# Four chained layers on one core: ScalarE evicts the first quarter of layer 0 ahead of rounding the shared gate weights, and VectorE rounds the shared up weights

## The reference

```
x = x + (x @ W_base.T + b_base + 2 * sum_e cond[b,e] * (x @ A_e.T) @ B_e.T)      # layer 0
x = x + x @ (sum_g cond[b,g] * weight_g * mask).T + bias                           # layer 1
x = x + sum over the top 2 experts e of cond[b]: w[b,e] * mlp_e(x)  + mlp_shared(x) # layer 2
x = x + (silu(x @ up_e.T + b) * (x @ gate_e.T + b)) @ down_e.T + b                 # layer 3, e = argmax cond[b]
mlp(x) = (gelu(x @ gate) * (x @ up)) @ down,   gate, up: 128x512, down: 512x128
```

## Time and profile before

| | |
|---|---|
| median of 3 runs | 85.93 us (85.29 to 86.2) |
| the profiled execution | 85.2 us, its span 83.9 us |
| PE busy in the span | 97% |
| DVE, ACT, POOL busy | 58%, 38%, 19% |
| granted TensorE clock | 1.000 of full speed in the whole span |

### The profile page before, as it was taken

How to read it: one execution, slowest core, us unless ns; L and a number is a source line. 1 busy time by engine, 2 the same in 40 slices (tenths; PEclk the granted TensorE clock), 3 DMA queues, 4 the chain that set the end, 5 groups by cost and what they waited for, 6 DMA issues and landing times.

```text
span 83.9 us, 1937 instructions
## 1 busy us (share of the span) xinstructions
PE 81.0 (97%) x620; PEld 77.0 (92%) x620; DVE 48.5 (58%) x115; ACT 31.5 (38%) x59; POOL 15.8 (19%) x20
## 2 busy tenths in 40 slices
PE   6999999999999999999999999999999999999990
PEld 6979988888889989999999999999999999999980
DVE  1489699754337996437438428446465564652271
ACT  6500996865558301122121221221302402316560
POOL 3020577589666600000000000000000000000000
DMA  1997000899990000985869899889899889805202
GB/s 21 334 392 279 2 0 0 240 413 390 420 388 35 0 0 15 308 272 182 314 220 323 238 324 331 277 264 309 268 368 336 311 308 311 331 19 120 99 0 66
DMA packets 5336, 18.51 MB, mean 221 GB/s; under 512 B 592, under 2 KB 1744, under 8 KB 5328
## 3 DMA queue, kind: packets, MB, share of 16 engines
q1 hardware_dynamic: 5040, 17.62, 61.1%
q10 hardware_dynamic: 288, 0.79, 2.4%
HBM read 17.88 MB, written 0.52 MB: 219 GB/s over the span
## 4 chain that ended last, share of the span: by engine, by line
PE 97%; DVE 0%; issue 0%; DVEq 0%
PE bank L690 34%; PE bank L700 17%; PE bank L713 9%; PE bank L727 5%; PE bank L662 4%; PE bank L654 4%; PE bank L670 4%; PE bank L586 3%; PE bank L592 3%; PE bank L622 2%; PE bank L677 2%; PE bank L678 2%; PE bank L680 2%; PE bank L610 2%; PE bank L601 2%; DVE out_sb L507 0%
## 5 line engine op out<-in xcount | busy, mean ns | idle before, releaser
L690 PE MATMUL bank<-x_t,pair_w 128*128 128x128 f32 (+1 forms) x256 | 31.0, 275 | 0.0
L690 PEld LDWEIGHTS bank<-x_t,pair_w 128*128 128x128 f32 x256 | 29.9, 192 | 0.1
L301 ACT ACTIVATE gelu<-bank 128x512 f32<-128x512 f32 x24 | 14.2, 598 | 31.6 <-PE bank L690 27.8
L478 DVE SCALAR_TENSOR_TENSOR hid<-gelu,wsel,bank 128x512 f32<-128x512 f32 x16 | 12.0, 748 | 18.5 <-PE bank L690 18.5
L700 PE MATMUL bank<-hid,pair_w 128*128 128x128 f32 x128 | 16.9, 275 | 0.0
L700 PEld LDWEIGHTS bank<-hid,pair_w 128*128 128x128 f32 x128 | 15.6, 192 | 0.1
L265 POOL TENSOR_TENSOR hid_l<-hid,hid_h 128x512 fp32r<-128x512 f32 x8 | 10.2, 1284 | 4.2 <-ACT hid_h L329 4.2
L476 DVE TENSOR_TENSOR hid<-gelu,bank 128x512 f32<-128x512 f32 x8 | 5.5, 688 | 6.1 <-ACT gelu L301 3.6
L713 PE MATMUL bank<-x_t,w 128*128 128x128 f32 x64 | 8.5, 276 | 0.0
L713 PEld LDWEIGHTS bank<-x_t,w 128*128 128x128 f32 x64 | 7.8, 192 | 0.0
L305 ACT ACTIVATE tanh<-half 128x256 f32<-128x256 f32 x6 | 2.5, 417 | 10.0 <-DVE half L514 10.0
(11 more groups left out here) (70 smaller groups left out, 76.4 us busy)
## 6 DMA issues: line engine op xcount, KB each, us to landing
pair_w<-in_skill SPq DMA_DIRECT2D x16, 768.0 KB, 5.5
w<-in_layer SPq DMA_DIRECT2D x8, 384.0 KB, 5.2
rest_sb<-in_rest SPq DMA_DIRECT2D x1, 661.0 KB, 3.9
x_t<-in_x SPq DMA_DIRECT2D x1, 512.0 KB, 5.4
shared_sb<-in_shared ACTq DMA_DIRECT2D x1, 512.0 KB, 5.2
out_x<-out_sb SPq DMA_DIRECT2D x8, 64.0 KB, 4.1
shared_sb<-in_shared ACTq DMA_DIRECT2D x1, 256.0 KB, 5.4
head_sb<-in_head SPq DMA_DIRECT2D x1, 164.0 KB, 2.3
```

What stands on the lines that cost most here:

```text
L301: act.activation(gelu[:, n, :], ps[:, :], ACT.Gelu_apprx_tanh).then_inc(gelu_ready, 1)
L478: dve.scalar_tensor_tensor(hid[:, n, :], gelu[:, n, :], wsel[:, bass.DynSlice(weight, 1)], u_ps[n][:, :], ALU.mult, ALU.mult).then_inc(hid ...
L690: mm = pe.matmul(ps[:, S * t:S * (t + 1)], pair_w[:, slot, n, 128 * t:128 * (t + 1)], x2_t[:, columns(b)], start=True, stop=True)
```

## The change

Three edits. On ACT, the eviction of quarter 0 stands before the rounding of the gate weights, which now stands between quarters 0 and 1; the rounding of the up weights leaves ACT. On DVE, a `tensor_copy` from `shared_sb` to `shared_h` does it, behind the last instruction of the routing and before the first `stream2`. The semaphore `sh_high`, which counted three roundings of one engine, becomes three semaphores, one for each block.

```diff
-        sh_high, sh_low = sem("sh_high"), sem("sh_low")
+        sh_high, sh_low = [sem(f"sh_high{n}") for n in range(3)], sem("sh_low")
...
-                    pool.wait_ge(sh_high, n + 1)
+                    pool.wait_ge(sh_high[n], 1)
...
-                    act.activation(shared_h[:, n, :], shared_sb[:, n, :], ACT.Copy).then_inc(sh_high, 1)
+                    act.activation(shared_h[:, n, :], shared_sb[:, n, :], ACT.Copy).then_inc(sh_high[n], 1)
...
+                act.wait_ge(rest_landed, 16)
+                stream1(0)
                 round_shared(0)
-                act.wait_ge(rest_landed, 16)
-                for n in range(4):
+                for n in range(1, 4):
                     stream1(n)
-                round_shared(1)
                 round_shared(2)
...
                 rank_second()
+                dve.wait_ge(gate_up_in, 16)
+                dve.tensor_copy(shared_h[:, 1, :], shared_sb[:, 1, :]).then_inc(sh_high[1], 1)
...
-                        pe.wait_ge(sh_high, m + 1)
+                        pe.wait_ge(sh_high[m], 1)
```

## The result

The changed kernel is **slower**: 86.44 us median of 22 runs (85.48 to 87.69), against 85.65 us of 22 runs of the kernel before (84.89 to 86.83). The ratio is **1.0098, 95% interval 1.0074 to 1.0123**, so about 0.8 us were lost, where 0.12 us were forecast as gained. A second measurement, 12 runs, gave 1.0072 (1.0025 to 1.0119).

The account below looks back on a forecast made before the run. PE, busy 97% of the span, was taken as the bound, so only holes could be closed: -0.14 us at the first seam, +0.02 at the next, 0 elsewhere, -0.12 us from the 85.93 median to 85.8 us; range 85.2 to 86.7.

Parts of the forecast that it names:

- the sum's last sentence: After the changed stretch all work is PE's own and shifts as a whole, so the -0.12 us reaches the end.
- The cast's price: Up rounding on DVE at one element per cycle, 0.69 us; lower bound 0.33 us at half streaming price.
- The first rival: The CAST on DVE waits behind POOL's first low part for the shared port: +0.7 us, about 86.6 us; chance 0.27.
- its dearer form: The CAST waits for POOL and still needs the full 0.53 us of streaming: +0.96 us.
- the rounding's end: ACT's gate rounding, put behind quarter 0's eviction, ends at 9.28, 0.12 us ahead of POOL's first low part; costs nothing.
- the first seam: Between layers 0 and 1 on PE, evicting quarter 0 first closes a hole: 0.14 us gained.
- the close fit of quarter 1: Quarter 1, ready at 9.65, is just in time for layer 1's fifth load at 9.77; a miss loses some hundredths.
- the zero for the semaphores: Three semaphores for one leave the waits and their places the same: no cost.
- The earlier up rounding: Up block ready at 10.18 instead of 10.97; POOL's second low part ends 0.36 us earlier, so PE's waiting load is freed.
- the third rival: Shared weights' DMA lands late in some runs, where the change saves more: up to 0.4 us, 85.5 us; chance 0.05.

Follow-up runs that it names:

- scalar_form: Changed kernel with VectorE's rounding of the up weights as a tensor_scalar (multiply by 1.0) instead of the cast: 86.44 us, ratio 1.0087.
- after_again: The changed kernel measured and traced again with no edit: 86.0 us, ratio 1.0072.
- pad_dve: Kernel before plus one 128x1 copy into a spare tile on VectorE, nothing else: 86.37 us, ratio 1.0071.
- dve_less: Changed kernel without one repeated wait (for base_ready) on VectorE, so its program there is as long as before: 85.89 us, ratio 1.0016.
- early_pad8: Changed kernel with the cast moved ahead of the routing's second half and eight more 128x1 copies on VectorE: 85.54 us, ratio 0.9974.
- cast_only: Kernel before with only the up rounding moved from ScalarE to VectorE (semaphore split), ScalarE still rounding the gate first: 86.58 us, ratio 1.0114.
- lost_less: cast_only without VectorE's repeated wait for base_ready, so its program there is as long as before: 86.08 us, ratio 1.0062.
- evict_only: Kernel before with only ScalarE's order changed, quarter 0 evicted ahead of the gate rounding; up rounding stays on ScalarE: 85.80 us, ratio 1.0008.
- split_only: Kernel before with only the semaphore sh_high split into three, no instruction moved: 85.60 us, ratio 1.0006.
- early_less: Changed kernel with the cast ahead of the routing's second half and without VectorE's repeated wait for base_ready: 85.54 us, ratio 1.0019.

## Why the prediction was wrong

**The step that failed is the sum's last sentence**: "All later work is PE's own, at full pace, and shifts as a whole." It is right for TensorE to within 0.1 us in most traces: from the expert matmuls to the last block its chain takes 54.84 to 54.96 us in fourteen of the sixteen, and 55.06 and 55.08 in scalar_form and after_again; why it is longer in these is open. It is wrong for the span, which ends with a store. I costed the added instruction by its time on VectorE and never by its place in the program. pad_dve shows that the mere instruction costs 0.6 us (1.0071), and dve_less that taking one away elsewhere brings the changed kernel back to 1.0016.

That the delay of the store is made by the code packet itself is read from the packets' records in all 16 traces, counted from the start of the last `out_sb`. In the seven with a last wait of 0.9 to 1.1 us, the packet starts at 1.47 us or later, or, in early_pad8, 0.85 us ahead of that `out_sb`, and the last data packet of the store ends at 1.55 in each. In the nine with 1.4 to 1.7 us, the packet starts at 1.06 to 1.41, and the store's last data packet ends at 1.80 to 2.13. In eight of these nine, exactly nine packets of the store end later than that, and the first of them starts within 0.02 us of the code packet's end; in cast_only, whose code packet was short (0.36 us), it is five. So, by its count and its start, the store's share on one DMA engine stood behind the code packet; the records do not name the engine. That makes 0.25 to 0.6 us; the wait grew by 0.1 to 0.3 us more, which no view explains. The packet was not moved by any other means than VectorE's program length.

**The cast's price** was mis-sized: 0.42 us, where I took 0.69 from the TENSOR_SCALARs of the earlier trace rows. Those rows misled. The one of 128 columns multiplies by a column from SBUF, the other is 16 wide, where half of the streaming time is 8 ns (the prediction's 0.53 us for 512 columns, scaled). A tensor_scalar of 512 columns with a constant ran at half price (scalar_form), so the argument that the fast form was off does not hold for an instruction with a constant. Whether the column from SBUF is what kept the rows at the full price was not tested.

**The first rival** had the mechanism: a cast that comes behind POOL waits for it and ends half of 0.53 us behind POOL's end. Forecast were 0.7 us (its dearer form adds up to 0.98, not 0.96); measured were 0.6 to 0.9 us of stage (lost_less, cast_only, after_again) and 0.54 us of time. That the measured 86.44 lies beside this rival's 86.6, and inside the range, is luck: most of it comes from the end of the span, for which no rival stood. What I had wrong is who comes first. POOL's first part needs both the routing and ACT's gate rounding, which the change itself puts later. I placed the rounding's end at 9.28; it came at 9.44 in the first trace, and POOL was level with the cast and lost. "Were the cast first, POOL would lose 0.2 us which it has" is wrong too: POOL lost 0.3 us, and the second low part and `x2_l` ended at 12.39 and 12.94, where 11.97 and 12.51 were forecast (0.1 us of both is the later start).

**Right** were the first seam (1.93 to 1.79 us), the close fit of quarter 1 (L624 has no hole), and the zero for the semaphores. The earlier up rounding bought next to nothing: L664 takes 1.01 us with it and evict_only's L663 1.04 without, and the stages are 17.90 and 17.91.

**The gain itself was read from one execution.** Between the first loads of layers 0 and 1 lie 1.78 or 1.79 us in all eleven traces with the eviction first. In the five with the old order it is 1.79 twice (pad_dve, lost_less), 1.88 (cast_only), 1.93 (before) and 2.06 (split_only): a hole of 0 to 0.27 us. In four of these ScalarE's gate rounding, which waits for the weights' DMA, starts 0.66, 0.78, 0.82 and 0.95 us behind the first load of layer 0, and the hole grows just so, 0, 0.09, 0.14 and 0.27; in pad_dve the two start together. So the edit takes away a wait that depends on when the weights land, as the third rival has it, and 0.14 us is the value of one trace.

So the 0.8 us are, as far as is known: about 0.6 us for the code load on the last store, which is in all nine traces with the longer program; 0.6 to 0.9 us of stage in the executions where the cast loses the race (one trace of three of this kernel), less some 0.05 to 0.1 us gained in the others. How often the cast loses in the timed runs was not measured.

## What to carry to other kernels

Read a gap in more than one execution before its removal is priced. Read the end of the span as its own stage: who waits for the last store, and which instruction packets fall on it; an instruction added to VectorE's program, or taken out of it far ahead of the end, moved one onto the store or off it here, so a result under 1% needs a control that changes the program's length and nothing else. A cast or tensor_scalar with a constant from SBUF to SBUF on VectorE is cheap (0.42 us for 512 columns) but takes turns with GpSimd for whole instructions, so put it where GpSimd is idle by order, not by luck. early_pad8 and early_less, which do both, are 1.1 and 0.7 us under the changed kernel by their ratios and cannot be told from the kernel before; no version was shown to beat it.

## What the runs showed of the hardware

- One instruction packet of queue q14 (8 KB, 0.31 to 0.64 us) among a store's 144 packets comes with nine of them (five in cast_only) held until it is through, and with a wait 0.5 to 0.8 us longer (SP's last wait 1.4 to 1.7 us in nine traces against 0.9 to 1.1 in seven).
- VectorE's CAST and TENSOR_SCALAR of 128x512, 32-bit, SBUF to SBUF: 0.42 us alone; 1.46 us behind a GpSimd instruction that started 0.09 us earlier. Recorded level with GpSimd's or 0.01 us later (five traces), they won, and GpSimd's took 1.56 in place of 1.26 us. The rule of the Trainium skill (SBUF — State Buffer, "Who interferes with whom"), that the first to start keeps the pair for the whole instruction, is borne out, with starts in the records too coarse to tell the winner at 0.01 us.
- `chosen` on GpSimd took 0.53 us beside VectorE's `x_l`, and 0.20 us in after_again, where it ended as `x_l` began.
